# Holding the gathers of a graph-attention kernel until a weighted sum is done

## The reference

```
h = max(layernorm(x), 0) @ W
e = leaky_relu(h @ a_src [:, None] + h @ a_dst [None, :], 0.2)
e = where(adj > 0, e, -9e15)
out = x + softmax(e, axis=1) @ h
```

## Time and profile before

| | |
|---|---|
| median of 3 runs | 804.69 us (803.43 to 808.2) |
| span of the profiled execution | 858.3 us |
| VectorE busy | 592.4 us (69%) |
| ScalarE busy | 525.0 us (61%) |
| GpSimd busy | 512.0 us (60%) |
| TensorE busy | 445.4 us (52%) |
| moved by DMA | 299.31 MB, mean 349 GB/s |

### The profile page before, as it was taken

One profiled execution on the slowest core, in us unless ns is written; L12 is line 12 of the kernel. 1 busy time (PEld: TensorE's weight loads), 2 busy tenths in 40 slices (PEclk: granted clock), 3 DMA queues, 4 the chain that ended last, 5 costly groups with the idle time before them and its releaser, 6 DMA issues.

```text
span 858.3 us, 8941 instructions
## 1 busy us (share of the span) xinstructions
PE 445.4 (52%) x1823; PEld 213.9 (25%) x1855; DVE 592.4 (69%) x3125; ACT 525.0 (61%) x371; POOL 512.0 (60%) x522
## 2 busy tenths in 40 slices
PE   4787555555555546545554545475055567533421
PEld 3652222222222222212122222132022222211221
DVE  7956577777777767566678767767177788755784
ACT  3979777666767667766387777666154877732000
POOL 3745666666656665765655666667636665665571
PEclk9888678677676777766677777777578767765555
DMA  8999999999999999989599999999659799992110
GB/s 339 424 370 419 404 408 408 408 411 407 410 409 409 408 409 405 399 315 393 217 415 411 408 409 408 408 401 409 233 210 394 277 408 409 411 402 92 25 38 11
DMA packets 40903, 299.31 MB, mean 349 GB/s; under 512 B 11052, under 2 KB 14034, under 8 KB 24464
## 3 DMA queue, kind: packets, MB, share of 16 engines
q1 hardware_dynamic: 22976, 276.83, 79.3%
q0 software_dynamic: 15328, 17.58, 6.6%
q10 hardware_dynamic: 2544, 4.33, 1.5%
HBM read 304.31 MB, written 8.65 MB: 365 GB/s over the span
## 4 chain that ended last, share of the span: by engine, by line
DVE 72%; another core or an unknown queue 11%; issue 8%; PE 5%; ACT 2%; DMA 0%; POOLq 0%; DVEq 0%; ACTq 0%
DVE x_all L821 18%; DVE rest L638 5%; DVE words L636 5%; DVE words L640 4%; PE banks L1049 3%; DVE wf L666 2%; DVE top L680 2%; DVE top_bit L662 2%; DVE cand L676 2%; DVE cand L723 1%; DVE one_hot L768 1%; DVE e L785 1%; DVE top_bit L672 1%; DVE top L727 1%
## 5 line engine op out<-in xcount | busy, mean ns | idle before, releaser
L361 POOL DMA_INDIRECT gathered<-table,index x448 | 448.7, 1002 | 295.1 <-DVE index L714 151.4
L467 ACT ACTIVATE mask_buf<-adj_buf,minus_half 128x2048 bf16<-128x2048 int32 x252 | 489.5, 1992 | 141.3 <-issue 56.5
L1049 PE MATMUL banks<-mask_buf,bit_ident 128*128 128x512 bf16 x992 | 316.6, 472 | 37.6 <-issue 24.7
L821 DVE SCALAR_TENSOR_TENSOR x_all<-gathered,weight,x_all 128x128 f32<-128x128 f32 x512 | 157.5, 348 | 16.1 <-DVE x_all L821 7.6
L1049 PEld LDWEIGHTS banks<-mask_buf,bit_ident 128*128 128x128 bf16 x1024 | 113.2, 121 | 203.4 <-issue 137.6
L1061 PE MATMUL banks<-is_wide,before 128*128 128x1 bf16 x64 | 6.9, 176 | 207.9 <-DVE is_wide L751 155.9
L1090 PE MATMUL banks<-x_all,one_hot 128*128 128x128 f32 x128 | 35.4, 368 | 74.1 <-DVE x_all L821 39.0
L481 ACT ACTIVATE prob<-e 128x16 f32<-128x16 f32 x31 | 6.5, 208 | 103.6 <-issue 72.7
L636 DVE MAX8 words<-banks 128x8 f32<-128x512 f32 x64 | 44.3, 693 | 25.4 <-PE banks L1049 18.7
L1061 PEld LDWEIGHTS banks<-is_wide,before 128*128 128x128 bf16 x64 | 4.5, 112 | 227.8 <-DVE is_wide L751 170.8
L640 DVE MAX8 words<-rest 128x8 f32<-128x512 f32 x64 | 44.5, 695 | 2.4 <-DVE rest L638 0.2
(11 more groups left out here) (162 smaller groups left out, 589.4 us busy)
## 6 DMA issues: line engine op xcount, KB each, us to landing
adj_buf<-in_adj SPq DMA_DIRECT2D x128, 2048.0 KB
gathered<-table,index POOLq DMA_INDIRECT x448
table<-gathered ACTq DMA_DIRECT2D x4, 1040.0 KB, 14.0
x_all<-in_x SPq DMA_DIRECT2D x3, 1024.0 KB, 10.8
out<-x_all SPq DMA_DIRECT2D x2, 1280.0 KB
x_all<-in_x SPq DMA_DIRECT2D x2, 512.0 KB, 5.1
out<-x_all SPq DMA_DIRECT2D x1, 1024.0 KB
w_gathered<-table,w_index POOLq DMA_INDIRECT x24
```

Source lines behind the costliest of these rows:

```text
L361: nc.gpsimd.indirect_dma_start(g_cols[buf][:, k, :], None, table, bass.IndirectOffsetOnAxis(index[:, buf, k:k + 1], 0), bounds_check=N, oo ...
L467: nc.scalar.activation(mask_buf[:, u], adj_buf[:, u], ACT.Sign, bias=minus_half[:]).then_inc(mask_ready, 1)
L821: ins = v.scalar_tensor_tensor(at[b], g_view[par][b][:, k, 0:F], weight[:, b, k:k + 1], at[b], ALU.mult, ALU.add)
L1049: ins = mm(bank, bit_ident[:, h * PART_BITS + c], mask_buf[:, u, c * BIT_COLS:(c + 1) * BIT_COLS], start=False, stop=(h == PARTS - 1 and c ...
```

## The change

For batches 2 to 27 (`DELAYED`) GpSimd waits for `out_ready` to be i-1 before it issues the gathers of batch i, that is for the weighted sum of batch i-2. VectorE computes that sum in its iteration i+1, behind `decode(i)` in iteration i. The wait for the buffer is contained in it. Batches 0, 1 and 28 to 31 stay as they were, and so do the number and kind of all instructions.

```diff
+DELAYED = range(SUM_LAG - 1, BY_TILE[0] - 2)
...
             def gather_batch(i):
                 buf = i % BUFS
-                if i >= BUFS:
+                if i in DELAYED:
+
+                    pool.wait_ge(out_ready, i - SUM_LAG + 2)
+                elif i >= BUFS:
                     pool.wait_ge(out_ready, i - BUFS + 1)
                 if i == LAST:
                     pool.wait_ge(index_ready, indexed(i, 1))
```

## The result

The changed kernel takes 1004.29 us, median of 4 runs (1001.71 to 1007.72), against 804.89 us before: a ratio of 1.2477, 95% interval 1.245 to 1.2504. The forecast of slower was right, and the time lies in the range, 34 us over the predicted 970.

A forecast was written before the change was run, and what follows sets the result against it. The prediction took the ring of gathers and weighted sum as the new bound: 26 turns of 29.2 us plus 9 make 768, plus 236.2 outside them 1004 us in the profile, and 970 us in the median, range 895 to 1035.

The forecast's parts named there:

- The bound before: Main loop before the change: DMA share 1.01 at 409 GB/s from 135 to 270 us; a batch takes 22.16 us.
- The ring: Sum's end, release 0.85, gather issue 17.98, landing L, logits and sum 6.40 us: 29.2 us for each of 26 batches.
- The landing L: Time from the end of a batch's gather issue until the last gather lands: taken as 4.0 us.
- The wide gathers, 9 us: Wide gathers behind batches 12 and 22 run beside the sum and slow it by 4.5 us, twice.
- Decode freed of its stalls: VectorE's decode loses its stalls beside gathers, up to 5 us a batch, but this gives nothing to the end.
- The faster rival: Freed decode counts and gathers fit: all 26 turns take 22.16 us, 761 us in the median; chance 0.03.
- From the trace to the median: Profiled 1004 us becomes 941 if the excess stretches everything, 1004 if lost inside the turns; middle 970 taken.
- the front: The part of the kernel in front of the 26 turns, taken as unchanged.
- the stretch behind the turns: The part behind the sum of batch 26, taken as unchanged at 113 us.
- Quick landing: Rival: rings are quiet when the last gathers land, L 0.9 us, a turn 26.1, say 895 us; chance 0.12.
- VectorE was never late: Rival denied here: decode stalls through the whole run, a turn is 34 us, 1057 to 1128 in the median; chance 0.06.
- The wait was not met already: Rival denied here: GpSimd's new wait is already met, so the time stays at 805 us; chance 0.02.

The follow-up runs named there:

- The first trace: The kernel before, unchanged, as profiled for the prediction: 858.3 us, 53.6 us longer than the median.
- The second trace: The kernel before, unchanged, traced once more: 804.93 us, span 803.1.
- logits behind the sum: The changed kernel with the logits of batch i-2 moved behind the weighted sum of batch i-3, all gathers and new waits kept: 804.63 us.
- 7, 10 gathers: The changed kernel with only 7, or only 10, of the 14 gathers of each batch up to 29 kept: 783.83 us and 886.77 us.
- half the loads: The changed kernel with half of each adj load left out from batch 1 on: 917.45 us.
- release at the logits: The changed kernel with the gathers of batch i released by the logits of batch i-1, not by the end of the weighted sum: 906.49 us.
- seven gathers, no new wait: The kernel before with 7 of the 14 gathers of each batch up to 29 left out: 778.15 us.

## Why the prediction was right, point by point

- **The bound before.** Right: the loads, 22 us a batch with a DMA share of 1.01, in both traces. The first trace alone shows it less well than the prediction says: over all 26 turns its share is 0.95, and the chain on its page is mostly VectorE:

```profile
DVE 72%; another core or an unknown queue 11%; issue 8%; PE 5%; ACT 2%; DMA 0%; POOLq 0%; DVEq 0%; ACTq 0%
```

  The second trace has DMA for 68% of it.
- **The ring.** Right in each piece: 0.85, 17.98 and 6.40 were predicted, 0.78, 17.91 and 6.38 measured. Its signs are there too: line 789 waits some 12 us in each turn, GpSimd 12.31 us for line 825, runs start 30 us apart, and the DMA share is 0.77. Opening it (logits behind the sum) gave everything back, and shortening it (7, 10 gathers, an earlier release) gave back what the pieces say, less what the landing took.
- **The landing L.** The term that was mis-sized. I took 4.0 us between 0.9 and 5.1; it was 5.14 in the turn shown and 5.3 in the mean of 26, over the 5.1 that I had allowed at most. The mean turn was 30.5 us in place of 29.2, 35 us in all. Two things were off: I ended it with the last packet, and VectorE starts 0.7 to 1.2 us later (packets of the gathers' queue were seen until between 390.0 and 390.5, line 789 starts at 391.16); and the rings' idle time comes behind the landing, not at it. By stretch, issue, landing, and logits with the sum in the turn shown (the share of the DMA engines is the last but one column):

```profile
368.10:386.00 17.90, 13.70 (x52) 6.32 (x50) 10.56 (x64) 10.19 (x6) 13.93 (x14) 0.70 0.99 395
386.00:391.00 5.00, 0.16 (x1) 0.00 (x0) 0.00 (x0) 0.00 (x0) 0.01 (x1) 0.80 0.55 217
391.00:398.30 7.30, 0.71 (x4) 0.71 (x4) 6.76 (x28) 5.16 (x4) 0.00 (x0) 0.50 0.31 101
```

  The 2 us of the Trainium skill ("DMA: Bandwidth & Descriptors", section "Anatomy of one DMA") are near the run with half the loads (1.4 us from the end of the last issue, 2.4 from its start) and far under the turns shown in which the rings were loaded (5.1 to 6.6).
- **The wide gathers, 9 us.** Not there. A sum in a run of 37 gathers (427.80 to 475.68 us) took 6.5 us. The 10.9 us of the earlier trace rows were, like the stalls of decode, of that one execution. And the 23 gathers of such a batch take 23 x 1.30 = 29.9 us to issue, which just fits into a turn of 30.5. Where turns are shorter it does not: with half the loads (26.6 us in most turns) and with the release at the logits, the turn behind the first wide gathers took 30.0 and 30.1 us.
- **Decode freed of its stalls.** The term was put at nothing, which was right: VectorE waits in each turn anyway. But the 5 us it was to free do not exist, as there are no such stalls outside the first trace. The faster rival rested on them alone and falls with them.
- **From the trace to the median.** Of the first trace's 55.2 us over the second, 38.4 lie in the 26 turns, 13.9 behind them and 2.9 in front. The changed kernel's trace, 1005.9 us, has none of it, as its own median is 1004.29. So nothing was to be taken off for it, and halving the way between 941 and 1004 is what put the forecast 34 us low. That its upper end, 1004, is the measured time owes something to luck: against it L adds 35, the wide gathers take off 9, the front 2 and the stretch behind the turns 22 (113.0 to 91.0), which leaves the 1005.9 of the span.
- **The rivals.** Quick landing needs quiet rings; half the loads gave 1.4 us and 917 us. VectorE was never late: it waited in each turn. The wait was not met already.

## What to carry to other kernels

When a producer is to start later, look for the ring and not for the slack alone: find what releases it, what waits for its result, and whether that wait stands ahead of the releasing instruction in the same queue. If it does, no turn can be shorter than release, issue, landing and the consumer's work together. Here that is 30.5 us where 22.4 bound before, and moving the wait behind the release removes it; with 7 gathers it is 22 us and costs 0.9%. And where a trace stands 7% off the median, take a second one before a term is built on its stalls.

## What the runs showed of the hardware

- A run of gathers lands 1.6 us behind its issue (median of 26 turns) with a DMA share of 0.53 over the turns, 5.1 us with 0.77, and 5.9 to 6.3 us with 0.87 to 1.00: in these runs most of a gather's latency comes from the loads around it.
- GpSimd issues an indirect DMA each 1.30 us (1.00 and 0.30), beside VectorE's decode, beside its weighted sum and with VectorE idle alike.
- Decode, for its part, is hardly slowed by gathers: 4.22 us without any (seven gathers, no new wait), 4.47 us where the gathers run beside it (369.49 to 373.96 us in the changed kernel).
